# Masking the diagonal score tiles with a minimum on VectorE instead of a mask product on TensorE, with other waits at the stage borders

## What is computed

```python
xn = layernorm(x)                                  # x: 2 x 2048 tokens x 1024, eps 1e-5, no scale
q, k, v = xn @ wq, xn @ wk, xn @ wv                # 32 query heads, 8 key/value heads, 32 wide
scores = einsum('bihd,bjhd->bhij', q, repeat(k, 4)) * 32 ** -0.5
scores = where(causal, scores, finfo.min)
s = softmax(scores) @ repeat(v, 4) @ wo            # attention and its output product
logits = xn @ W_router.T                           # 8 experts, the two best, renormalised: w
h = einsum('td,erd->ter', xn, lora_A)
g = silu(xn @ W_base.T + b_base + einsum('ter,eor,te->to', h, lora_B, w) * 2.0)
out = x + s * g
```

## Time and profile before

| | |
|---|---|
| runs | 3310.94, 3310.89, 3309.64 us; median 3310.89 us |
| the profiled execution | 3312.78 us, its span 3311.0 us |
| granted TensorE clock over the span | 0.994 |
| busy share of the span | TensorE 98%, VectorE 57%, ScalarE 43%, GpSimd 41% |
| chain that ended last | TensorE 91%, VectorE 4%, ScalarE 1%, DMA 1% |
| stages on the time axis (us) | projection 0 to 676, attention 682 to 2559, then gate and output |

### The profile page before, as it was taken

The page is one execution under the profiler, slowest core; times in us unless marked ns, Lnnn a source line. Parts: engine busy times, 40 slices in busy tenths (PEclk is TensorE's granted clock), DMA queues, the critical chain, the costliest instruction groups (busy, mean ns, idle before and its releaser), DMA issues.

```text
span 3311.0 us, 51264 instructions
## 1 busy us (share of the span) xinstructions
PE 3238.1 (98%) x18048; PEld 2193.0 (66%) x18048; DVE 1889.5 (57%) x4622; ACT 1437.3 (43%) x2658; POOL 1357.0 (41%) x549
## 2 busy tenths in 40 slices
PE   6999999999999999999999999999999999999999
PEld 5888888755555555555555555555553788888887
DVE  6333333577777777777777777777773322223333
ACT  3222111056666666666666666666666111010110
POOL 0000000046776776776686677678667000000000
PEclk9999999999999999999999999999999999999999
DMA  6455554556666666566566666666666544445554
GB/s 232 158 163 158 166 159 147 143 119 132 143 137 135 143 130 138 125 142 138 128 145 138 137 136 129 138 132 145 135 162 142 174 140 138 144 156 191 192 199 165
DMA packets 283503, 494.53 MB, mean 149 GB/s; under 512 B 40864, under 2 KB 156576, under 8 KB 263328
## 3 DMA queue, kind: packets, MB, share of 16 engines
q1 hardware_dynamic: 260256, 333.04, 33.7%
q0 software_dynamic: 20736, 151.00, 23.2%
q10 hardware_dynamic: 2304, 7.87, 0.7%
HBM read 205.03 MB, written 134.74 MB: 103 GB/s over the span
## 4 chain that ended last, share of the span: by engine, by line
PE 91%; DVE 4%; ACT 1%; DMA 1%; issue 1%; SPq 1%; POOL 0%; ACTq 0%; DVEq 0%; POOLq 0%
PE cols_ps L1380 16%; PE o_ps L1335 15%; PE rows_ps L1284 14%; PE cols_ps L596 4%; PE cols_ps L598 4%; PE cols_ps L597 4%; PE cols_ps L1353 4%; PE rows_ps L795 4%; PE rows_ps L796 4%; PE rows_ps L797 4%; PE rows_ps L947 4%; PE rows_ps L946 4%; PE rows_ps L945 4%; DVE row_max L1469 2%; PE cols_ps L1383 2%; PE o_ps L596 1%
## 5 line engine op out<-in xcount | busy, mean ns | idle before, releaser
L1249 POOL TENSOR_TENSOR added<-added,probs 128x2048 f32<-128x2048 f32 (+3 forms) x320 | 1171.7, 3661 | 859.2 <-PE o_ps L1335 793.0
L1469 DVE TENSOR_REDUCE row_max<-rows_ps 128x1 f32<-128x512 f32 x1536 | 994.8, 683 | 297.8 <-PE rows_ps L1284 294.7
L1441 ACT ACTIVATE probs<-cols_ps 128x512 f32<-128x512 f32 x1728 | 919.1, 610 | 305.6 <-PE cols_ps L1380 278.6
L1473 DVE CUSTOM_DVE_ANT_0 masked_rows<-rows_ps,tri 128x128 bf16<-128x128 f32 (+3 forms) x1024 | 484.5, 483 | 176.7 <-PE rows_ps L1284 174.1
L1284 PE MATMUL rows_ps<-k_st,q_st 96*128 96x512 f32 (+3 forms) x1536 | 520.7, 362 | 12.8 <-DVE row_max L1469 7.9
L1380 PE MATMUL cols_ps<-q_st,k_st 97*128 97x512 f32 x1248 | 519.8, 423 | 6.7 <-issue 6.1
L1335 PE MATMUL o_ps<-probs,v_st 128*32 128x512 f32 (+3 forms) x4224 | 428.6, 522 | 0.0
L1380 PE MATMUL cols_ps<-q_st_last,k_st 97*128 97x512 f32 x928 | 381.3, 425 | 4.4 <-ACT dma_added L1441 3.2
L1284 PE MATMUL rows_ps<-k_st,q_st_last 96*128 96x512 f32 (+3 forms) x1024 | 364.5, 381 | 2.0
L1380 PEld LDWEIGHTS cols_ps<-q_st,k_st 97*128 97x128 f32 x1248 | 236.7, 190 | 179.7 <-issue 113.0
L1284 PEld LDWEIGHTS rows_ps<-k_st,q_st 96*128 96x128 f32 x1536 | 292.7, 191 | 91.0 <-DVE row_max L1469 36.9
(11 more groups left out here) (130 smaller groups left out, 3862.7 us busy)
## 6 DMA issues: line engine op xcount, KB each, us to landing
dma_added<-probs POOLq DMA_DIRECT2D x144, 1024.0 KB, 7.8
q_st<-scratch_q_hi SPq DMA_DIRECT2D x96, 256.0 KB, 6.0
x_sb<-in_x SPq DMA_DIRECT2D x32, 512.0 KB, 4.1
scratch_xt_hi<-xt_hi SPq DMA_DIRECT2D x32, 512.0 KB, 6.0
scratch_xt_lo<-xt_lo SPq DMA_DIRECT2D x32, 512.0 KB, 6.7
scratch_q_hi<-out_hi SPq DMA_DIRECT2D x64, 256.0 KB, 2.5
scratch_q_lo<-out_lo SPq DMA_DIRECT2D x64, 256.0 KB, 2.9
l_sb<-scratch_l_inv SPq DMA_DIRECT2D x256, 64.0 KB, 4.8
```

What stands on the lines that cost most here:

```text
L1249: nc.gpsimd.tensor_tensor(total[:, :, q0:CH], total[:, :, q0:CH], probs_of(c, j)[:, :, q0:CH], ALU.add).then_inc(pool_added, 1)
L1441: nc.scalar.activation(probs_of(c, j)[:, :, i * P:(i + 1) * P], cols_ps[cols_slot(AT_T[t])][:, :].rearrange("p (h q) -> p h q", h=NREP), A ...
L1469: nc.vector.tensor_reduce(into, bank[:, :], AX.X, ALU.max).then_inc(rows_free, 1)
L1473: nc.vector.tensor_tensor_reduce(masked_rows[rows_slot(k)][:, 0:keys], bank[:, 0:keys], tri[:, CH - keys:CH], 1.0, MASKED, ALU.add, ALU.ma ...
```

## The change

1. The mask product L1383 is gone. VectorE gets a new kind "X" in the table, one per diagonal tile: it waits for `cols_full` of the tile and takes the elementwise minimum of the bank and the mask (allowed places hold 3.0e38, masked ones -1.0e38), in place. ScalarE waits for `masked_ready` before the exponential of a diagonal tile. `stage` puts an X behind the row scores of its tile.
2. The constants are made inside the stages' block (`constants_programs`); SyncE and ScalarE no longer wait for them.
3. The first chunk's 4 products for v and the router run with k outermost, each k waiting for its own low piece; TensorE's program has the first pair of chunks unrolled and a loop over the next two.
4. Row scores in the last projection chunk begin one product later and go 9 per product; k is loaded before q, v after q; the last q chunk of group 0 is loaded before the end of the projection.
5. At the projection's end TensorE no longer waits for everything: it starts the first tiles when all but the last two accumulators are free, and waits for these before tile 2; the wait for the second row of ones moves to group 1; the wait for the projection's stores moves to group 1 on SyncE.
6. `first_products` of the gate makes all products with high weights first, waiting for `w_hi_ready`, then those with low weights.

```diff
+SEEN = 3.0e38
-SCORES_OF = KT
+SCORES_OF = KT + 1
...
+for _t, (_c, _j, _i) in enumerate(TILES):
+    if _j == TPC * _c + _i:
+        event(_t, "X", _c, _j)
...
+def constants_programs(nc, ident, mask_ji, tri, made):
+    def gpsimd(pool):
+        for m, value in ((ident[:, :], 0.0), (tri[:, :], 0.0), (mask_ji[:, :, :], SEEN)):
+            nc.gpsimd.memset(m, value).then_inc(made, 1)
...
+    def vector(dve):
+        dve.wait_ge(made, 5 + NREP)
+    def tensor(pe):
+        pe.wait_ge(made, 5 + NREP)
...
-        pe.wait_ge(w_lo_ready, KT)
...
+                if first_pair and u == 0:
+                    pe.wait_ge(acc_free, TPC)
+                    for k in range(KT):
+                        pe.wait_ge(w_lo_ready, k + 1)
+                        (wh, wl) = weights(k, C_V, C_Q)
+                        for t in range(TPC):
+                            (th, tl) = tokens(k, t * P, (t + 1) * P)
+                            into = acc[t][:, C_V:C_Q]
+                            nc.tensor.matmul(into, th, wh, start=(k == 0), stop=False)
...
-                    scored = SCORES_OF * (j - 1)
+                    scored = SCORES_OF * (j - 2)
...
+        for k in range(NW):
+            pe.wait_ge(w_hi_ready, k + 1)
+            for part in range(2):
+                for half in range(2):
+                    nc.tensor.matmul(acc[half][:, :], tokens[0][:, part, k, :], w[:, k, 0, halves[half]],
+                                     start=(k == 0 and part == 0), stop=False)
         for k in range(NW):
             pe.wait_ge(w_lo_ready, k + 1)
...
-            pe.wait_ge(project.acc_free, project.acc_free_last)
-            pe.wait_ge(ones_ready, 2)
+            pe.wait_ge(project.acc_free, project.acc_free_last - 2)
+            pe.wait_ge(ones_ready, 1)
...
-                        diagonal = j == TPC * c + i
...
-                        ins = nc.tensor.matmul(into, k_st[n.u][:, j * P:(j + 1) * P], q_st[c][:, :, i * P:(i + 1) * P],
-                                               start=True, stop=not diagonal)
-                        if diagonal:
-                            ins = nc.tensor.matmul(into, ident_r[:, :], mask_ji[:, :, :], start=False, stop=True)
-                        ins.then_inc(cols_full, 1)
+                        nc.tensor.matmul(into, k_st[n.u][:, j * P:(j + 1) * P], q_st[c][:, :, i * P:(i + 1) * P],
+                                         start=True, stop=True).then_inc(cols_full, 1)
...
                         act.wait_ge(cols_full, cols_count(n, AT_T[t]))
+                        if j == TPC * c + i:
+                            act.wait_ge(masked_ready, n.lin(TPC * CPB, j + 1))
...
+                    elif kind == "X":
+                        cc, back, j = op[1:]
+                        u = AT_T[TILES.index((cc, j, j - TPC * cc))]
+                        dve.wait_ge(cols_full, cols_count(n, u))
+                        bank = cols_ps[cols_slot(u)][:, :].rearrange("p (h q) -> p h q", h=NREP)
+                        nc.vector.tensor_tensor(bank, bank, mask_ji[:, :, :], ALU.min).then_inc(masked_ready, 1)
```

More of the change, by code:

```diff
@@ L371, in pair_of_chunks @@
                     store_xt(Step(pair, 1) if u == 0 else Step(pair + 1, 0), 1 - u)
+                if last and u == 1:
+                    wait_apart(sp, acc_full, NA * NCH - 1, passed)
+                    wait_apart(sp, xt_stored[1], 16 * 2 * TPC * (NCH // 2 + 1), passed)
+                    load_last()
                 s = (NO * u + NO - 1) % 2
@@ L605, in tensor, with pair_of_chunks @@
             turn(zero, j)
-        pe.wait_ge(w_lo_ready, KT)
-        def pair_of_chunks(pair, b, last):
+        def pair_of_chunks(pair, first_pair, last):
             for u in range(2):
@@ L620, in pair_of_chunks @@
                 pe.wait_ge(turn_free, n.lin(NTR, NTR + 4))
-                for t in range(TPC):
+                if first_pair and u == 0:
[7 more added lines that the diff above has]
+                            nc.tensor.matmul(into, th, wh, start=(k == 0), stop=False)
+                            nc.tensor.matmul(into, th, wl, start=False, stop=False)
+                            ins = nc.tensor.matmul(into, tl, wh, start=False, stop=(k == KT - 1))
+                            if k == KT - 1:
+                                ins.then_inc(acc_full, 1)
+                for t in () if first_pair and u == 0 else range(TPC):
                     pe.wait_ge(acc_free, n.lin(NA, t + 1))
@@ L630, in pair_of_chunks @@
                     pe.wait_ge(acc_free, n.lin(NA, item + 1))
-                    scored = SCORES_OF * (j - 1)
-                    between = None if ahead or j == 0 else lambda k: scores_to(scored + k + 1)
+                    scored = SCORES_OF * (j - 2)
+                    between = None if ahead or j < 2 else lambda k: scores_to(scored + k + 1)
                     product(acc[item % 4][:, :], lambda k: weights(k, c0, c0 + P), tokens, between).then_inc(acc_full, 1)
@@ L636, in pair_of_chunks @@
                         turn(m, j)
-                    if not ahead and j > 0:
+                    if not ahead and j > 1:
                         scores_to(scored + SCORES_OF)
@@ L809, in first_products @@
         pe.wait_ge(t_loaded[0], 64)
+        halves = [slice(half * HALF, (half + 1) * HALF) for half in range(2)]
+        for k in range(NW):
[4 more added lines that the diff above has]
+                                     start=(k == 0 and part == 0), stop=False)
         for k in range(NW):
@@ L812, in first_products @@
             for half in range(2):
-                ins = step(0, half, k)
+                ins = nc.tensor.matmul(acc[half][:, :], tokens[0][:, 0, k, :], w[:, k, 1, halves[half]], start=False,
+                                       stop=(k == NW - 1))
                 if k == NW - 1:
@@ L952, in output_programs, with all_stages @@
     return Output(load_first, load_second, loads_and_stores, first_high, highs, first_low, finishes, products)
-def all_stages(nc, x, wall, sc, ident, ident_r, mask_ji, tri, wb, lb, b_base, wo, out):
+def all_stages(nc, x, wall, sc, ident, mask_ji, tri, wb, lb, b_base, wo, out):
     ctx = ExitStack()
@@ L1057, in all_stages @@
         NW = KT + 1
+        made = sem("made")
+        constants = constants_programs(nc, ident, mask_ji, tri, made)
         project = project_programs(nc, ctx, x, wall, sc, ident, work, small, cols_ps + [o_ps], rows_ps)
@@ L1160, in load_ahead @@
                 load_q(0, 2)
+                load_v(0, 0)
             moved = [0]
             def move_rows(end):
-                for k in FIRST_ROWS[moved[0]:end]:
+                for k in FIRST_ROWS[moved[0]:max(end, 0)]:
                     if ROWS[k][0] == "M":
@@ L1184, in run @@
                             wait_apart(sp, probs_ready, made_count(n, c - 1, 0, NJG) if c else n.lin(NUG, 0), passed)
-                        if c == 0 or not last_group:
+                        if c == 0 and n.lin(1) == 1:
+                            project.all_stored(sp)
+                        if c == 0 and n.lin(1) == 0:
+                            pass
+                        elif c == 0 or not last_group:
                             load_q(n.lin(1, 0 if c == 0 else 1), (c - 1) % CPB)
@@ L1273, in run @@
                             .then_inc(norm_ready, 1)
+            constants.gpsimd(pool)
             project.gpsimd(pool)
@@ L1297, in scores_to @@
             def scores_to(end):
-                for k in FIRST_ROWS[scored[0]:end]:
+                for k in FIRST_ROWS[scored[0]:max(end, 0)]:
                     free = rows_free_count(None, 0, k) if k >= NROWS else None
@@ L1372, in run @@
                         t, j, i = op[1:]
+                        if n.lin(1) == 0 and t == 2:
+                            pe.wait_ge(project.acc_free, project.acc_free_last)
+                        if n.lin(1) == 1 and t == 0:
+                            pe.wait_ge(ones_ready, 2)
                         if (j, i) == (0, 0):
@@ L1493, in maxima_to @@
             def maxima_to(end):
-                for k in FIRST_ROWS[done[0]:end]:
+                for k in FIRST_ROWS[done[0]:max(end, 0)]:
                     count = rows_count(None, 0, k)
@@ L1504, in maxima_to @@
                 done[0] = max(done[0], min(end, len(FIRST_ROWS)))
+            constants.vector(dve)
             project.vector(dve, begin_maxima, maxima_to)
```

70 lines of the change are left out of this document (33 added, 37 removed).

## The result

| | before | with the change |
|---|---|---|
| median of the runs | 3310.9 us | 3456.4 us (3450.2 to 3460.3) |
| ratio, 95% interval | | 1.044 (1.042 to 1.045) |
| profiled execution, span | 3311.0 us | 3455.4 us |
| granted TensorE clock over the span | 0.994 | 0.974 |

Slower, as forecast, but by 145 us where the forecast had 72, and above the top of the range (3440). The spans differ by 144.4, and the starts of the transposed-score matmuls (L1380 before, L1460 now) divide that: up to the first tile of the attention -8.6 (681.6 to 673.0), the first fifteen groups +152.0 (1757.8 to 1909.8), the last group +7.0 (111.9 to 118.9), behind the last tile -6.0 (759.7 to 753.7).

The account below looks back on a forecast made before the run. TensorE was taken as the bound, the change as decided by the minimum's path. 3312.8 (profiled execution) + 84 (stalls) - 12 (borders) = 3385, or 3383 us against the median; range 3312 to 3440.

Parts of the forecast that it names:

- Where it is decided: Diagonal tiles p (a chunk's first), p+4, p+7, p+9: p+7 waits for p+4's minimum behind row maxima; chunk 2 stall 1.5 us.
- the wait for q and its half clock: Last projection chunk: the 4.9 us wait goes, and 6.7 us at half clock behind it, worth 3.4; net -8.3.
- rival 2: Steady attention: stalls make the clock fall, some 1.6 us each, +32 to +96; time 3405 to 3450 us; chance 0.2.
- the stalls: Diagonal tiles of fifteen groups: 1.4 us lost per chunk after the saved mask products, 5.6 per group, +84 in all.
- the bank shift behind the previous group's p+9: Chunk 3's p+9 is followed at once by the next group's diagonal tile (0, 0); bank count shifts, costing 0.6 us more.
- The last group: Sixteenth group: TensorE waits for ScalarE at nearly every tile, the mask products lie in that wait; 0 counted.
- The borders: Start, last projection chunk, attention's start and gate together: -12 us.
- start and last chunk: Projection: start no longer waits for the constants, net -2.5 us; last chunk loses its wait for q, net -8.3.
- the attention's start: First tiles issue three earlier, but the fourth waits for the first minimum behind a 1.76 us memset; net -1 us.
- The gate: TensorE's wait of 5.0 us, ending at 2559.32, is the token load's, so high weights first gain 0.
- Rival 1: Diagonal tiles: three banks cover the minimum, p+7 stalls at most 0.5 us; time 3243 to 3275 us; chance 0.18.
- Rival 3: Diagonal tiles: only the first stall counts, catch-up costs nothing; 3317 to 3335 us, to 3350 with part of the second; chance 0.15.

Follow-up runs that it names:

- `fill`: The change plus repeated row-score products (mostly 2560 columns) on TensorE ahead of each p+7, where it would stand still; 3411.6 us, 1.030.
- `min_first`: The change with each minimum ahead of the row maxima of its own tile in VectorE's order; 3333.6 us, 1.006.
- `borders_only`: The change without part 1: mask product back on TensorE, no minimum, parts 2 to 6 kept; 3301.7 us, 0.996.
- `borders_no_gate`: `borders_only` with part 6 (the gate's high weights first) taken back; 3303.6 us.
- `min_only`: The kernel before with part 1 alone: minimum on VectorE, no mask product, no border change; 3464.5 us, 1.046.
- `min_first_not1`: The change with p+4 masked by a product, p, p+7 and p+9 by the minimum, ahead of their tile's row maxima; 3295.0 us, 0.995.
- `min_not1`: The change with p+4 masked by a product, the other three diagonal tiles by the minimum in the change's order; 3337.4 us, 1.007.

## Why the prediction was outside its range

**Right.** Where it is decided (p+4 to p+7, VectorE's list in order), the minimum's 0.69, the 2.8 us from p+4 to p+7 in chunk 2, the exponential that waits for the minimum, the wait for q and its half clock gone (forecast -8.3; the traces show -7.6, from 5.3 us late at 360 us to 2.3 early at the last product of the projection). The steady group without a fall, forecast at 122 to 124, took 124.1.

**The step that failed: the sum held no clock.** I had the price of a fall (1.6; measured 1.5) and the rule behind it, but I put it into rival 2 with a chance of 0.2, because in the kernel before only the last group showed falls. The stall I forecast was itself new: before, TensorE hardly stood still in the steady groups (0.3 us at a time at most), so their clean clock said nothing of a kernel with 60 pauses ahead of p+7, nearly all of 1.05 to 1.65 us. 32 of the 60 brought a fall: +44 us in groups 1 to 14. The section of the Trainium skill that rival 2 cited ("TensorE: Matmul & The Clock Gate", on a second HAM failure mode) has the clock oscillate under frequent small pauses of this kind; here the trace of the change agrees, with 32 falls behind such pauses. `fill` showed that with those pauses filled the falls go; this term belonged in the sum. Neither this term nor the next would have left my range alone: 3383 + 44 = 3427 and 3383 + 18 = 3401. Both together, 3445, do.

**A term mis-sized: the stalls, 84 forecast, 102 found.** Cut into four stretches with one diagonal each (the cuts lie at tiles 20, 50 and 100 of a group), the group grew by 2.66, 1.68, 1.66 and 0.82. I had 1.4 as mean. Chunk 2, which I counted step by step, had p+12 1.58 later against p+4 where I had 1.44. The first stretch is the miss: in chunk 0 the next four tiles after p, which I priced at 0.6 for the bank shift behind the previous group's p+9, came 0.91 later, and the group's own stall between p+4 and p+7, 1.8, lay only a few tiles on, with no W between to win anything back.

**The last group, 0 forecast, +7.0 found.** I read it as waiting for ScalarE at nearly every tile and took that as cover. The trace of the kernel before says otherwise: up to the end of chunk 2 the sixteenth group keeps step with the fifteenth within 0.4 us, its row scores run until 2499.2, and the waits for ScalarE come behind that, in chunk 3. So the first three chunks pay like those of any group: at the end of chunk 2 the change is 8.2 us late there, with three falls, and `fill` 6.2, with one that begins only 3 us ahead of that point. Chunk 3 gives some back, and both the clock and the order count: the whole group is 7.0 us longer in the change, 3.6 in `fill`, 0.2 in `min_first`.

**The borders, -12 forecast; -11 by the traces of `borders_only` and before.** The sum was right by luck, its terms were not. In `borders_only` the last product of the projection comes 3.3 us earlier (forecast 10.8 for start and last chunk), the attention's start gains 2.0, the last group 2.1, and the stretch behind the last tile 3.7. In the change the start was to gain 2.5 and had lost 5.3 by 360 us (part 3). The attention was to gain 1. In the change its first three tiles follow the projection at once (tile 0 comes 0.03 us behind the last product there, 6.33 before), then tile 3 waits 4.9 for ScalarE, which waits for the first minimum; tile 20 comes 24.5 us behind that product, 23.4 before. Without the minimum, in `borders_only`, it is 21.3, a gain of 2.1. The gate: I read TensorE's wait of 5.0 as the token load's; `borders_no_gate` shows it was VectorE's low parts, as the profile's own label said. It is -6.0 in the change, not 0, most of it by the minimum's own delay, as `min_only` shows.

**The rivals.** Rival 1, the banks cover the minimum, is refuted for this order, and p+4 was not covered in the better order either: in `min_first` TensorE still idles 0.43, 0.89, 0.73 and 0.48 us ahead of p+7. Rival 3 fell too: the catch-up is there. Rival 2 was the case; the time lies above its 3405 to 3450 because the stalls beneath it were larger too. My range ended at 3440, below that rival's own top.

## What to carry to other kernels

An operation moved to an engine with time to spare is priced by its place in that engine's list: look at what stands ahead of it and how soon its bank is wanted again. Move single instances, not all: four of sixteen carried nearly the whole loss here, and eight others (p and p+7, with the minimum ahead of the row maxima) brought a gain. And when a forecast contains regular pauses of TensorE that the old kernel did not have, the old kernel's clean clock is no evidence; put the falls into the sum.

## What I had not expected of the hardware

- TensorE became faster by being given more work: products of no use, worth 68 us in the kernel before, took 45 us off the time of the changed one, by the clock alone.
- A tile that had to wait slows what follows it. In the timeline above the row score comes 0.34 behind the tile that waited (1260.83, 1261.17) where it came 0.24 behind p+4 (1258.00, 1258.24). In steady group 4 the distances from a tile to its row score are 1.3 us more in sum than before, a tenth of a microsecond at each of twelve tiles. It is a part of why estimates of mine that added up the visible waits fell short by 1 to 2.3 us per group (`min_first_not1`, `min_not1`).
- With the first pair of chunks unrolled (part 3), TensorE paused for 1.65 and 2.35 us where it enters the loop and then ran 3.4 us at half clock, in the middle of a stage that ran without a pause there before. The cause of the second pause is open.
